# Cross-attention scores three steps ahead, hidden rows on ScalarE, and one-run layouts for its queries, keys and values

## The reference, cut to what matters

```python
x = x + attn(layernorm(x))          # self-attention, 224 x 224 scores per head
x = x + xattn(layernorm(x), ctx)    # cross-attention, 224 x 750 scores per head:
#   rel    = |k - q - (750 - 224)|
#   scores = q k^T / sqrt(32) - slope[head] * rel
#   out    = softmax(scores) v @ Wo + bo
x = x + moe(layernorm(x))           # softmax router, top 2 of 8, silu(a) * b experts
```

## Time and profile before

| | |
|---|---|
| median of 3 runs | 1738.88 us (1736.13 to 1742.64) |
| the profiled execution | 1741.56 us, span from first to last instruction 1739.8 us |
| PE busy | 1661.7 us, 96% of the span |
| DVE, ACT, POOL busy | 62%, 43%, 43% |
| TensorE clock granted, mean | 0.985 of full speed |
| DMA moved | 309.50 MB, 178 GB/s over the span |

### The profile page before, as it was taken

The page is one execution under the profiler, slowest core; times in us unless marked ns, Lnnn a source line. Parts: engine busy times, 40 slices in busy tenths (PEclk is TensorE's granted clock), DMA queues, the critical chain, the costliest instruction groups (busy, mean ns, idle before and its releaser), DMA issues. The chain is left out here.

```text
span 1739.8 us, 34540 instructions
## 1 busy us (share of the span) xinstructions
PE 1661.7 (96%) x10934; PEld 1334.2 (77%) x10934; DVE 1079.5 (62%) x1897; ACT 748.1 (43%) x1348; POOL 754.5 (43%) x845
## 2 busy tenths in 40 slices
PE   9898999999999989899999989899999999999998
PEld 8786787888787767677777766678888888888876
DVE  6554566565656567788888888664564646436653
ACT  4224344444434427566565554523442424224441
POOL 3200423332333318788787665531451514215441
PEclk9999999999999999999999998899999999999999
DMA  7747665666666749998777874247564646356773
GB/s 243 254 152 218 179 191 173 193 195 208 180 187 198 189 119 184 206 208 169 151 158 149 172 153 152 87 125 232 182 185 149 196 128 220 102 163 186 244 245 91
DMA packets 207936, 309.50 MB, mean 178 GB/s; under 512 B 21592, under 2 KB 151336, under 8 KB 202944
## 3 DMA queue, kind: packets, MB, share of 16 engines
q1 hardware_dynamic: 188304, 227.16, 48.8%
q0 software_dynamic: 14768, 46.27, 10.8%
q10 hardware_dynamic: 4752, 34.61, 5.4%
HBM read 224.30 MB, written 83.66 MB: 177 GB/s over the span
## 5 line engine op out<-in xcount | busy, mean ns | idle before, releaser
L2216 DVE TENSOR_REDUCE part_max<-a_s_bank 112x1 f32<-112x500 f32 (+1 forms) x368 | 224.6, 668 | 62.9 <-PE a_s_bank L1936 49.2
L2111 ACT ACTIVATE a_prob<-a_st_bank 125x448 f32<-125x448 f32 x384 | 196.8, 546 | 112.2 <-PE a_st_bank L1959 94.7
L2922 DVE TENSOR_TENSOR e_u_sb<-e_u_bank,e_b_row 128x512 f32<-128x512 f32 x134 | 92.2, 688 | 230.4 <-PE e_u_bank L2679 217.8
L2677 PE MATMUL e_u_bank<-e_w_hi,e_xT_hi 128*128 128x512 f32 x536 | 214.3, 400 | 0.9 <-DVE e_w_lo L2915 0.4
L2678 PE MATMUL e_u_bank<-e_w_lo,e_xT_hi 128*128 128x512 f32 x536 | 209.9, 392 | 0.0
L2679 PE MATMUL e_u_bank<-e_w_hi,e_xT_lo 128*128 128x512 f32 x536 | 209.5, 391 | 0.0
L2738 ACT ACTIVATE e_g_hi<-e_g_bank 128x256 fp32r<-128x256 f32 x133 | 51.3, 385 | 342.5 <-PE e_g_bank L2686 340.5
L2839 POOL DMA_INDIRECT out<-l_rows,e_y_row x33 | 53.0, 1605 | 291.2 <-DVE l_rows L2965 148.5
L1786 POOL TENSOR_TENSOR a_part_sum<-a_prob 125x448 f32<-125x448 f32 x128 | 147.5, 1157 | 31.7 <-ACT a_prob L2111 31.4
L1028 POOL TENSOR_TENSOR m_prob_sum<-m_prob 112x224 f32<-112x224 f32 x128 | 93.9, 738 | 138.2 <-ACT m_prob L1270 130.0
L2815 POOL TENSOR_TENSOR e_w_lo<-e_w_raw,e_w_hi 128x1024 fp32r<-128x1024 f32 x28 | 102.6, 3674 | 48.9 <-ACT e_w_hi L2748 48.9
(11 more groups left out here) (438 smaller groups left out, 4309.9 us busy)
## 6 DMA issues: line engine op xcount, KB each, us to landing
e_w_raw<-L_ffn_Wl SPq DMA_DIRECT2D x96, 512.0 KB, 8.4
e_b_row<-L_ffn_bl ACTq DMA_DIRECT2D x33, 1024.0 KB
m_c_in<-ctx POOLq DMA_DIRECT2D x12, 1000.0 KB, 6.1
k<-m_kt_hi SPq DMA_DIRECT2D x48, 250.0 KB, 3.3
k<-m_kt_lo SPq DMA_DIRECT2D x48, 250.0 KB, 4.1
v<-m_cv SPq DMA_DIRECT2D x48, 224.0 KB
a_v_sb<-v SPq DMA_DIRECT2D x32, 336.0 KB
m_q_st<-q SPq DMA_DIRECT2D x93, 112.0 KB, 3.0
```

Source lines behind the costliest of these rows:

```text
L2111: act.activation(prob[s % 2][:, hh, 2 * u:2 * u + 2, :], st_bank[n % SB][0:CR, 0:2 * S].rearrange("p (e q) -> p e q", e=2), ACT.Exp).then_ ...
L2216: dve.tensor_reduce(out, scores, AX.X, ALU.max).then_inc(s_free, 1)
L2677: pe.matmul(out, xT_hi[:, slot, k, :], w_h, start=(k == 0), stop=False)
```

## The change

In the opening POOL waits for the value projections of later chunks before it issues the loads of `m_wv`, `m_wq` and the context. In DRAM, `q2`, `k2` and `v2` become one contiguous run for each partition and load: q 3584 B instead of 4 runs of 896 B, k 12000 B instead of 4 runs of 3000 B, v 3072 B instead of 6 runs of 512 B. For that the columns of the cross-attention's weights are permuted within each group on the host, the stores of keys are cut where a batch ends (16 of 48 blocks now take 4 stores instead of 2), and the stores of values write 4 runs of 512 B instead of one of 2048 B. In the cross phase the first scores go one step further ahead (s + 3; step 3 is added to loop 0), the row maxima are transposed in the middle of the loop, after `hh == 1`, and ACT copies them there; the 4 filler matmuls at s = 31 are dropped. The normalised rows are made by ACT (`hidden_rows`), from a shift and a scale that DVE prepares (`inverse`). The load of the output weights (1 MB) and bias moves on SP behind the loads of step 5.

```diff
@@ opening_phase, pool
                 load_x(3)
+                pool.wait_ge(o_free, prod_at["wv", 1, TT - 1] + 1)
                 load_w_behind("m_wv", "wo")
+                pool.wait_ge(o_free, prod_at["wv", 2, 0] + 1)
                 load_w_behind("m_wq", "m_wk")
+                pool.wait_ge(o_free, prod_at["wv", 2, TT - 1] + 1)
+                pool.sem_inc(turn, 1)
                 pool.dma_start(c_in[:, :, :], ctx[0]).then_inc(ctx_loaded, DMA)
@@ middle_phase, sync
+    def pieces(ch):
+        cuts = [CN * ch] + [CTX * b for b in range(1, B) if CN * ch < CTX * b < CN * ch + CN] + [CN * ch + CN]
+        return [(a // CTX, a % CTX, a - CN * ch, z - CN * ch) for a, z in zip(cuts, cuts[1:])]
-                            sp.dma_start(k2[m, part, :, CN * ch:CN * ch + CN], as_f32(tile[:, i, :])).then_inc(k_stored[i], DMA)
+                            for b, col, a, z in pieces(ch):
+                                sp.dma_start(k2[m, part, b, :, col:col + z - a], as_f32(tile[:, i, a:z])).then_inc(k_stored[i], DMA)
-                            sp.dma_start(v2[r0 + a:r0 + z, :], cv[a:z, i, :]).then_inc(cv_stored[i], DMA)
+                            sp.dma_start(v2[b, :, a:z, t, :].rearrange("g p d -> p g d"), cv[a:z, i, :].rearrange("p (g d) -> p g d", g=GROUPS)).then_inc(cv_stored[i], DMA)
@@ cross_phase, sync
-                        sp.dma_start(as_f32(k_st[i][rows, :, :]), k[g, k_part, :, CTX * b:CTX * b + CTX]
-                                     .rearrange("(h p) t -> p h t", p=DH)).then_inc(qk_loaded[i], DMA)
+                        sp.dma_start(as_f32(k_st[i][rows, :, :]), k[g, k_part, b].rearrange("(p h) t -> p h t", p=DH)).then_inc(qk_loaded[i], DMA)
-                sp.dma_start(w_raw[:, :, :], w_out.rearrange("(k p) n -> p k n", p=P)).then_inc(w_loaded, DMA)
+                    if s == 1:
+                        sp.dma_start(w_raw[:, :, :], w_out.rearrange("(k p) n -> p k n", p=P)).then_inc(w_loaded, DMA)
@@ cross_phase, tensor
+    def first_step(s):
+        step = s + 2 if s < 1 else s + 3
+        return step if step < STEPS else None
-                    elif s == 31:
-                        keep_clock(bank, 4)
-                    if s + 2 < STEPS:
-                        turn_max(s + 2)
                     pe.wait_ge(sum_done, sums_before(s + 1))
-                            if s + 2 < STEPS and n in first_units(s + 2):
-                                first_scores(s + 2, hh, n)
+                            if first_step(s) is not None and n in first_units(first_step(s)):
+                                first_scores(first_step(s), hh, n)
+                        if s >= 1 and s + 2 < STEPS and hh == 1:
+                            turn_max(s + 2)
+                    if s == 0:
+                        for hh in range(2):
+                            for n in range(RP):
+                                first_scores(3, hh, n)
+                    if s < 1:
+                        turn_max(s + 2)
...
@@ cross_phase, scalar
+                def hidden_rows(b, t):
+                    act.wait_ge(shift_ready, b + 1)
+                    act.activation(xh[b % 2][:, t, :], x_new[:, t, :], ACT.Identity, bias=shift[:, t:t + 1], scale=rstd[:, t:t + 1]).then_inc(h_ready, 1)
+                        if s >= 1 and s + 2 < STEPS and hh == 1:
+                            query_rows(s + 2)
+                        if hh < 2 and batch_at(s, 2) is not None:
+                            hidden_rows(batch_at(s, 2), hh)
@@ cross_phase, vector
+                def inverse(b):
+                    dve.wait_ge(std_done, b + 1)
+                    dve.reciprocal(rstd[:, :], std[:, :]).then_inc(rstd_done, 1)
+                    dve.wait_ge(rstd_done, b + 1)
+                    dve.scalar_tensor_tensor(shift[:, :], mv[:, :, 0], -1.0, rstd[:, :], ALU.mult, ALU.mult).then_inc(shift_ready, 1)
-                        if hh % 2 == 0 and batch_at(s, 2) is not None:
-                            hidden(batch_at(s, 2), (hh // 2,))
+                    if batch_at(s, 1) is not None:
+                        inverse(batch_at(s, 1))
```

More of the change, by code:

```diff
@@ L765, in unit_of, with key_stores @@
         return n // CU, n % CU
+    def pieces(ch):
+        cuts = [CN * ch] + [CTX * b for b in range(1, B) if CN * ch < CTX * b < CN * ch + CN] + [CN * ch + CN]
+        return [(a // CTX, a % CTX, a - CN * ch, z - CN * ch) for a, z in zip(cuts, cuts[1:])]
+    def key_stores(n):
+        return sum(2 * len(pieces(k // KT)) for k in range(n % RING, n, RING))
     def blocks_at(s, hh):
@@ L945, in load_cross @@
                         rows = slice(DH * r, DH * r + DH)
-                        for part_of, dram, part, n in ((tile_q, q2, q_part, S), (tile_k, k2, k_part, CTX)):
-                            sp.dma_start(as_f32(part_of[rows, :, :]), dram[g, part, :, 0:n].rearrange("(h p) t -> p h t", p=DH)).then_inc(first_loaded[g], DMA)
+                        for part_of, dram, part in ((tile_q, q2, q_part), (tile_k, k2, k_part)):
+                            sp.dma_start(as_f32(part_of[rows, :, :]), dram[g, part, 0].rearrange("(p h) t -> p h t", p=DH)).then_inc(first_loaded[g], DMA)
                     sp.dma_start(as_f32(tile_k[KA:KA + 4, :, :]), k_lin[g].rearrange("h r c -> r h c")).then_inc(first_loaded[g], DMA)
@@ L1525, in cross_phase @@
                 note(s_at, "rank", s)
-        if s + 2 < STEPS:
+        if s < 1:
             note(st_at, "max", s + 2)
+        if s == 0:
+            for hh in range(4):
+                for n in range(RP):
+                    note(s_at, "s", 3, hh, n)
     for t in range(2):
@@ L2372, in _ @@
                             dve.tensor_tensor(w_lo[:, hh, :], w_raw[:, hh, :], as_f32(w_hi[:, hh, :]), ALU.subtract).then_inc(w_ready, 1)
[L2373 to L2374 removed]
+                        if first_step(s) is not None:
+                            maxima(first_step(s), hh)
                         if s == -1 and hh == 2:
@@ L2423, in _ @@
                             slots(28, hh - 2)
-                    if s + 2 < STEPS:
-                        row_maxima(s + 2)
+                    if first_step(s) is not None:
+                        row_maxima(first_step(s))
+                    if s == 0:
+                        for hh in range(4):
+                            maxima(3, hh)
+                        row_maxima(3)
                     if 1 <= s < STEPS - 1:
                         normalise(s - 1)
+                    if batch_at(s, 1) is not None:
+                        inverse(batch_at(s, 1))
                     if s == 11:
@@ L3168 @@
         arrays["L0_attn_" + n] = np.ascontiguousarray(w.transpose(2, 1, 0))
+    for name, cols in (("L0_xattn_Wkv", D), ("L0_xattn_bkv", D), ("L0_xattn_Wq", D), ("L0_xattn_bq", D)):
+        whole = arrays[name].copy()
+        heads = whole[..., 0:cols].reshape(whole.shape[:-1] + (GROUPS, 4, DH))
+        whole[..., 0:cols] = np.swapaxes(heads, -1, -2).reshape(whole.shape[:-1] + (cols,))
+        arrays[name] = whole
     d = {n: nc.dram_tensor(n, a.shape, F32, kind="ExternalInput").ap() for n, a in arrays.items()}
```

52 lines of the change are left out of this document (29 added, 23 removed).

## The result

The changed kernel takes **1718.58 us** (median of 6 runs, 1713.52 to 1721.10) against 1736.12 us for the kernel before in the same comparison (6 runs, 1729.55 to 1742.64): ratio 0.9894, 95% interval 0.9867 to 0.9921. That is 17.5 us less; 1714 us had been forecast. The profiled execution of the changed kernel has a span of 1715.0 us, 24.8 us less than that of before, where 25.1 had been summed. The medians are the measure, and 7.6 us of the forecast's 25.1 are missing in them.

A forecast was written before the change was run, and what follows sets the result against it. PE was taken as the bound: its work plus 78 us in which it stands still. Terms A to G summed to -25.1 us, so 1716.5 us for the profiled execution and 1714 us as median; range 1702 to 1729 us.

The forecast's parts named there:

- B: Cross-phase loops: transpose of the maxima leaves the value matmuls, 0.27 us in each of 29 loops; -7.8 us.
- C: Cross-phase loop ends: the next loop no longer waits for ACT's copy, 0.27 us in 24 loops; -6.5 us.
- A: Opening: later POOL loads no longer hold up a store of values, so DVE and PE wait less; -5.9 us.
- rival 2: Mid-loop in the cross phase: ACT or DVE takes PE's place, the copy is not covered; 1724 us, chance 0.24.
- D: Cross phase: long waits at the transpose of the maxima shrink and the fillers at s = 31 go; -4.8 us.
- E: Cross-phase loops with s % 4 == 2: hidden rows on ACT end PE's waits on DVE; -5.6 us.
- F: Start of cross phase: DVE paces loop 0's added scores, PE waits for step 6's load; +4 us, bounds -8 and +14.
- rival 4: Cross-phase key and query loads: the narrower window makes them late and the kernel slower; 1787 us, chance 0.05.
- Layouts: DRAM layouts: longer runs leave the rate of key and query loads to 32 partitions unchanged; only value loads gain.
- Rival 1: Start of cross phase: one-run loads go at 343 instead of 192 GB/s, ending step 6's wait; 1705 us, chance 0.17.
- G: Tail and stores: loop 29 paced by ACT, +1 us; 32 more stores and shorter runs in the middle phase, +0.5 us.

The follow-up runs named there:

- e8: Kernel before with only the opening's three POOL waits added: 1727.09 us against 1734.03, ratio 0.9971.
- e4: Changed kernel with ACT's copy filling one head instead of four from step 4 on, same place: one run, 1710.70 us.
- e2: Changed kernel with the transpose of the maxima and ACT's copy in row 3 instead of row 1: 1710.79 us, ratio 0.9868 to the kernel before.
- e1: The changed kernel measured again, unedited: 1721.97 us against 1732.77 for the kernel before, ratio 0.9916.
- e5: Changed kernel with the hidden rows computed on DVE again: 1729.26 us against 1734.03 for the kernel before, ratio 0.9976.
- e6: Changed kernel with output weights loaded after step 6's load and split in loop 4 instead of 3: 1717.34 us, ratio 0.9900 to the kernel before.
- e7: Changed kernel with the old DRAM layouts of queries, keys and values: 1721.47 us, ratio 0.9922 to the kernel before.
- e10: Changed kernel with the first scores of steps 2 and 3 begun half a loop earlier: 1721.72 us, ratio 0.9920 to the kernel before.
- e11: Changed kernel with the edits of e2, e6 and e10 together: 1711.29 us, ratio 0.9858 to the kernel before.

## Why the prediction was right, and where not

The time came out as forecast within 4.6 us, but not for the reasons given. The two largest terms, B and C, brought a third of what was counted. The absolute miss is no larger because the kernel before takes 2.8 us less in this comparison than the 1738.88 us from which the forecast started: that is luck.

**A, the opening (-5.9): right.** -5.7 in the profiles, -5.8 in e8 alone, with PE's 4.45 us wait gone and DVE's of 9.50 us for a store down to 1.9; in the profiles of all runs with this code the middle phase begins between 145.5 and 147.1 us (151.92 before). In e8's profile nothing of it is given back in the middle phase (493.42 us against 493.20).

**B and C, transpose and copy (-7.8 and -6.5): wrong by two thirds.** At the loop's end the change frees 0.69 us, more than the 0.54 counted. The step that failed is "three banks cover about 1.1 us. So one copy is covered", and with it the 0.13 us allowed for the transpose. The transpose and the copy use one of the three banks themselves. From the first score matmul behind the transpose (871.14) to PE's need of the bank (872.10) it is 0.96 us, and the copy starts 0.30 us into that: the cover is 0.66 us, the copy 0.91. PE waits 0.3 us. The transpose costs 0.19 us at its new place. 0.69 - 0.5 leaves 0.15 to 0.2 a loop, where 0.54 was counted: over 24 to 29 loops 8 to 10 us. A plain loop lasts 10.37 to 10.41 us, where 10.0 to 10.1 was named as the sign. This is rival 2's mechanism, on ACT's side, and for B and C more than its size (7 us); I had given it 0.24. Its whole price was 10 us, and what is missing is 7.6 us by the medians and 9.3 in the profiles against e8. So rival 2 describes what happened better than the forecast does, though 1718.6 us lies about midway between 1714 and its 1724. e4 takes the copy's length away and e2 its place; each gives back 0.3 to 0.4 us a loop.

**D, the long waits (-4.8): right in part.** Loops 5, 9 and 17 are 0.96 to 1.00 us shorter, 0.8 more than a plain loop (0.39 + 0.2 counted). Loop 29 is 3.7 us shorter than in e8, where 4.0 was counted: the fillers and the moved first scores. The other eight loops with routing are 1.3 us shorter than in e8, where 5.0 was counted, and B and C alone account for 1.4 us. So the 1.5 us that D had there did not come. That the step in hand took the waits of loops 5, 9 and 17 is argued; no run sets the window back alone.

**E, hidden rows (-5.6): the sum nearly, the place not.** The six loops are 5.7 us shorter than in e8, 1.1 of it by B and C: -4.6. But 5.0 of the 5.7 us are loop 22, which lasted 17.1 us at a granted clock of 0.80 in e8 and in before and lasts 12.1 us at 1.00 now, and 2.0 of that come back in loop 21 (19.93 us instead of 17.97; 18.22 in e1). Loops 6, 10 and 18 gained 0.3 us each, little more than B and C; loop 14 lost 0.2. The waits that the forecast read in loops 10, 14 and 18 were in part those of one profile: these loops last 13.72, 14.83 and 13.72 us in before but 12.74, 12.94 and 12.74 in e8, where the waits before the transposes come to 1.2 us instead of 2.9. ACT's waits are there, as forecast: in loop 6 0.27 and 0.40 us; the instruction takes 0.82 us, not 0.68. Undone alone (e5) the move costs 10 to 14 us, with half clock in three loops and DVE's instructions slower than before.

**F, the start (+4, bounds -8 to +14): right.** DVE paces loop 0 with two blocks of twelve maxima:

```profile
658.03 7.16 DVE L2255 TENSOR_REDUCE part_max<-a_s_bank 112x1 f32<-112x500 f32 x12 [2.49 <-PE a_s_bank L1961]
...
665.32 7.11 DVE L2255 TENSOR_REDUCE part_max<-a_s_bank 112x1 f32<-112x500 f32 x12
```

Loop 0 lasts 18.78 us (17 forecast, 18.7 with the 1.7 us for half clock), the wait for step 6 is 3.6 us (5 forecast), and no load is late by more behind it, so rival 4 is out. The stretch comes out at +5.9 us where 4 + 3.1 (the moved work) - 1.6 (B and C) = 5.5 was counted, and 1.1 us of it is B's and C's shortfall; in e1's profile it is +7.4. The term for half clock can't be checked by the granted clock. In loops -1 to 3 it withholds 8.5 us against 3.4 before, but loop 0 lasts 18.55 us at 0.91 (e6), 18.78 at 0.82 and 21.60 at 0.76 (e2).

**Layouts: weighed rightly.** The rate at the start is 189 GB/s from 673 to 695 us (178 and 201 in its halves), where 190 to 200 was foreseen for destinations of 32 partitions, and e7 shows the same rate with short runs. Rival 1 is out. The Trainium skill (SBUF — State Buffer, "Door 1: The DMA port swizzle") gives 189 GB/s at 1 MiB for partitions 0 to 31. The 189 and 191 GB/s measured here agree with it. The prediction's "whatever the runs" is not the page's, which goes by partitions and by the size of the transfer; that runs of 896 and 3000 B do as well as one is shown by e7.

**G and the sum.** The tail gave 0.5 us against e8; whether the middle phase changed can't be told (-1.1, in a spread of 6.5 us between profiles). Against e8 B and C were some 9 us too hopeful, of 9.3 us in all; the rest nearly cancels (E 1.0 and D's routing loops 1.5 short, the middle phase 1.6, the start 0.7, loops 5, 9 and 17 0.6 and the tail 0.5 better). The medians lack 7.6.

Two numbers of the prediction are slips without effect on the sum: rival 4's 1787 us is the forecast plus 73, where 73 less what A to E bring is 1781; and B's 0.27 us gives 2.42 us from the first value matmul to the first sum, not 2.45.

## What to carry to other kernels

When work is moved from a loop's end into its middle, price it by the buffers that are left while it holds its own, not by all of them, and count the time from its producer to the next claim on that buffer. Put a short transpose and its copy ahead of a block of matmuls that uses other banks. Where the DMA engines are at their full time in a start-up, look after each edit on PE or DVE whether the next wait for a load has taken it back, as in e10 and e11. And take a loop's waits from more than one profile before pricing them: here the same code showed 12.3 and 8.9 us.
